# Last layer's output of an FFT network: each 32-partition quadrant holds a quarter of an image's rows, and 40 output transfers stand in place of 64

## The reference, cut to what matters

```
z = conv3x3(x, K);  z = relu(batchnorm(z));  x = x + 0.1 * conv3x3T(z, K)
x = batchnorm(x)
xh = fft2(x);  x = real(ifft2(xh * t))        # t: one real table per layer
```

## Time and profile before

| what | value |
|---|---|
| median of three runs | 795.53 us |
| profiled execution, its span | 796.84 us, 795.0 us |
| PE (TensorE matmul) busy | 748.3 us (94%) |
| DVE busy | 497.3 us (63%) |
| ACT busy | 449.3 us (57%) |
| POOL (GpSimd) busy | 95.5 us (12%) |
| `out<-Z` transfers | 60 by SP, 4 by ACT, 64 KB each |
| written to HBM | 4.19 MB |

### The profile page before, as it was taken

The page is one execution under the profiler, slowest core; times in us unless marked ns, Lnnn a source line. Parts: engine busy times, 40 slices in busy tenths (PEclk is TensorE's granted clock), DMA queues, the critical chain, the costliest instruction groups (busy, mean ns, idle before and its releaser), DMA issues.

```text
span 795.0 us, 14900 instructions
## 1 busy us (share of the span) xinstructions
PE 748.3 (94%) x6016; PEld 375.6 (47%) x6016; DVE 497.3 (63%) x911; ACT 449.3 (57%) x703; POOL 95.5 (12%) x92
## 2 busy tenths in 40 slices
PE   4788999999999999999999999999999999999993
PEld 1222333222455875324558752345587632455782
DVE  2568787765957853449578534496686333966761
ACT  0456666636745765267357652683576625826773
POOL 0357766830000000000000000000000000000000
PEclk9789999999999999989999999899999998999997
DMA  9991111248000132830000328400004273000045
GB/s 184 189 153 28 28 29 28 55 91 187 2 1 1 33 77 68 193 98 2 1 1 18 93 57 191 112 1 1 2 7 103 55 183 88 1 1 2 1 100 113
DMA packets 60133, 51.16 MB, mean 64 GB/s; under 512 B 53153, under 2 KB 53282, under 8 KB 58018
## 3 DMA queue, kind: packets, MB, share of 16 engines
q1 hardware_dynamic: 54690, 48.92, 28.7%
q10 hardware_dynamic: 5376, 1.30, 1.1%
HBM read 11.92 MB, written 4.19 MB: 20 GB/s over the span
## 4 chain that ended last, share of the span: by engine, by line
PE 84%; DVE 8%; ACT 2%; issue 2%; DMA 1%; SPq 1%; POOL 0%; DVEq 0%; ACTq 0%; POOLq 0%
PE psum L873 40%; PE psum L1054 7%; PE psum L1025 7%; PE psum L947 6%; PE psum L1043 6%; PE psum L1009 5%; PE psum L896 3%; PE psum L998 3%; DVE spare L810 2%; PE psum L973 2%; PE psum L935 2%; DVE work L810 2%; PE psum L912 1%; DVE tabT L794 1%; PE psum L1018 1%
## 5 line engine op out<-in xcount | busy, mean ns | idle before, releaser
L873 PE MATMUL psum<-Z,wts 128*32 128x512 f32 x1536 | 176.7, 613 | 1.9 <-DVE Z L787 1.9
L873 PE MATMUL psum<-X,wts 128*32 128x512 f32 x1536 | 170.1, 593 | 0.2 <-DMA X<-X 0.2
L810 DVE COPY work<-psum 64x256 f32<-64x256 f32 x224 | 100.3, 448 | 22.8 <-PE psum L1009 15.9
L720 DVE BATCH_NORM_STATS2 stats<-Z 128x6 f32<-128x512 f32 x60 | 41.6, 693 | 102.2 <-ACT Z L470 101.8
L873 PEld LDWEIGHTS psum<-Z,wts 128*32 128x32 f32 x1536 | 48.9, 112 | 116.4 <-issue 107.8
L470 ACT ACTIVATE Z<-psum 128x512 f32<-128x512 f32 x64 | 38.2, 598 | 113.2 <-PE psum L873 102.1
L873 PEld LDWEIGHTS psum<-X,wts 128*32 128x32 f32 x1536 | 47.5, 109 | 105.4 <-issue 103.0
L555 ACT ACTIVATE work<-psum 64x256 f32<-64x256 f32 x160 | 83.1, 519 | 22.4 <-PE psum L1043 15.4
L530 ACT ACTIVATE Z<-Z,small 64x128 f32<-64x128 f32 (+3 forms) x92 | 84.8, 972 | 5.2 <-DVE small L778 4.7
L801 DVE SCALAR_TENSOR_TENSOR X<-psum,X 128x512 f32<-128x512 f32 x64 | 43.8, 684 | 46.6 <-PE psum L873 46.2
L542 ACT ACTIVATE work<-psum 128x512 f32<-128x512 f32 x64 | 61.1, 1108 | 8.9 <-PE psum L998 8.8
(11 more groups left out here) (104 smaller groups left out, 897.0 us busy)
## 6 DMA issues: line engine op xcount, KB each, us to landing
X<-X SPq DMA_DIRECT2D x64, 260.0 KB, 3.8
Z<-Z SPq DMA_DIRECT2D x32, 520.0 KB, 7.1
Z<-x SPq DMA_DIRECT2D x36, 128.0 KB, 4.8
out<-Z SPq DMA_DIRECT2D x60, 64.0 KB, 1.9
parS<-par SPq DMA_DIRECT2D x4, 673.0 KB, 8.2
Z<-x SPq DMA_DIRECT2D x12, 120.0 KB, 4.9
Z<-x ACTq DMA_DIRECT2D x14, 64.0 KB, 4.3
Z<-x SPq DMA_DIRECT2D x14, 64.0 KB, 4.6
```

Of the source, the lines that this page charges most:

```text
L810: last = nc.vector.tensor_copy(dst, src)
L873: last = nc.tensor.matmul(out_b[C * r:C * r + C, :], weights[:, o:o + C], rows(src, reg, bp, g, CH, dj - 1), start=(dj == 0), stop=(dj == ...
```

## The change

In the last layer only, quadrant r holds the 16 successive rows 16r to 16r + 15 of an image in place of every fourth row.

- `back_from_h` has another destination for the last layer: `backw` is laid out as (l, r, channel, part) with h = 16r + l. The same 64 elements of a copy now go out as 4 runs (r) of 16 elements (l), with 128 floats (512 bytes) between successive elements.
- `keep_invW` writes Z2 as (image, row l, column): an image's 16 rows of a quadrant lie together, 4 KB in a run.
- `store` sends, for each quadrant, n rows of one image as one run per partition, to a DRAM stretch that is one run too. Pairs 0 to 2 are sent whole (8 transfers of 128 KB for a pair, runs of 4 KB), after all four quarters. Pair 3 is sent in halves as before (64 KB, runs of 2 KB).

```diff
-        def planar(bp, p0=0, p1=128):
-            return Z2[p0:p1, bp * REG2:bp * REG2 + G * ROW].rearrange("p (g b w) -> p g b w", b=2, w=W)
+        def leaving(bp, image, l, n, p0=0, p1=128):
+            o = bp * REG2 + G * W * image + W * l
+            return Z2[p0:p1, o:o + W * n]
...
-        def back_from_h(n, bp, q):
+        def back_from_h(n, bp, q, last):
             src = bank(n).rearrange("p (c t h) -> p t c h", c=4, t=2)
             dst = backw[bp % 2][:, :].rearrange("p (h c e) -> p e c h", c=C // 2, e=2)[:, :, 4 * q:4 * q + 4]
+            if last:
+                src = bank(n).rearrange("p (c t r l) -> p t c r l", c=4, t=2, r=R)
+                dst = backw[bp % 2][:, :].rearrange("p (l r c e) -> p e c r l", r=R, c=C // 2, e=2)[:, :, 4 * q:4 * q + 4]
...
-        def store(eng, bp, image, g0, g1):
-            for r in range(R):
-                eng.dma_start(in_dram(out, 2 * bp + image, r)[:, g0:g1],
-                              planar(bp, C * r, C * r + C)[:, g0:g1, image]).then_inc(out_done, 16)
+        def store(eng, bp, image, l, n):
+            for q in range(R):
+                to = out[2 * bp + image].rearrange("c (q l) w -> q c (l w)", q=R)[q]
+                eng.dma_start(to[:, W * l:W * l + W * n],
+                              leaving(bp, image, l, n, C * q, C * q + C)).then_inc(out_done, 16)
...
-            for bp in range(BP):
-                for h in range(2):
-                    for q in range(2 * h, 2 * h + 2):
-                        bk.result(NUMBER["invW", DEPTH - 1, bp * Q + q])
-                    for image in range(2):
-                        if (bp, h, image) != (BP - 1, 1, 1):
-                            store(sp, bp, image, G // 2 * h, G // 2 * h + G // 2)
-            sp.wait_ge(out_done, 16 * 2 * B * R)
+            for bp in range(BP - 1):
+                for q in range(Q):
+                    bk.result(NUMBER["invW", DEPTH - 1, bp * Q + q])
+                for image in range(2):
+                    store(sp, bp, image, 0, G)
+            for h in range(2):
+                for q in range(2 * h, 2 * h + 2):
+                    bk.result(NUMBER["invW", DEPTH - 1, (BP - 1) * Q + q])
+                store(sp, BP - 1, 0, G // 2 * h, G // 2)
+                if h == 0:
+                    store(sp, BP - 1, 1, 0, G // 2)
+            sp.wait_ge(out_done, 16 * (2 * R * (BP - 1) + 4 * R))
...
                 if j == DEPTH - 1:
-                    dst = planar(c // Q)[:, CH * (c % Q):CH * (c % Q) + CH]
-                    src = bank(n).rearrange("p (g w b) -> p g b w", g=CH, b=2)
+                    both = Z2[:, c // Q * REG2:c // Q * REG2 + 2 * G * W].rearrange("p (b l w) -> p l b w", b=2, w=W)
+                    dst = both[:, CH * (c % Q):CH * (c % Q) + CH]
+                    src = bank(n).rearrange("p (l w b) -> p l b w", l=CH, b=2)
```

More of the change, by code:

```diff
@@ L553, in keep_moved @@
                 bk.full(n)
-                for dst, src in forth_from_w(n, c % Q) if stage == "fwdW" else back_from_h(n, c // Q, c % Q):
+                for dst, src in forth_from_w(n, c % Q) if stage == "fwdW" else back_from_h(n, c // Q, c % Q, j == DEPTH - 1):
                     last = nc.scalar.activation(dst, src, ACT.Identity)
@@ L596, in _ @@
                 bk.result(NUMBER["invW", DEPTH - 1, (BP - 1) * Q + q])
-            store(act, BP - 1, 1, G // 2, G)
+            store(act, BP - 1, 1, G // 2, G // 2)
         @block.vector
```

## The result

Six runs of the changed kernel took 790.25 to 792.25 us, median 791.08; six of the kernel before, measured with them, had a median of 795.77. The ratio of the two is 0.9936, with a 95% interval of 0.9914 to 0.9958. The direction was as forecast. The gain, 4.7 us by the medians, is half as large again as the 3.1 that I had given, and 0.9936 x 795.53 = 790.4 lies just under my range. A later comparison gave 0.9918 (0.9894 to 0.9942).

A forecast was written before the change was run, and what follows sets the result against it. SP's issue pace was taken as the bound on the kernel's end. Fewer issues 4.1, later start -1.34 and smaller hold 0.32 gave 3.1 us gained: 795.53 - 3.1 = 792.4 us, own range 791.5 to 793.3, whole range 790.7 to 795.2.

The forecast's parts named there:

- the later start: SP's first issue of pair 2 waits for four quarters, not two: 779.25 in place of 777.91, costing 1.34 us.
- the copies with the wide stride: Last layer's 64 invH copies, now writing 512 bytes apart: 0 extra, at most 61 ns a copy.
- the Z2 writes: Writes into Z2 with runs of 64 floats on both sides: 0 extra, 777 ns with or without gaps.
- the data: 2.1 MB of pairs 2 and 3 through the DMA engines from 779.25: no cost, at most 0.2 us.
- Rival 4: Strided invH copies on DVE and ACT slow down; at twice the time 5.9 us slower, 801.4; chance 0.06.
- Rival 2: Larger transfers issue or move more slowly, 0.64 us per issue; gain only 0.5 to 2.1 us; chance 0.18.
- A hold that moves: Instruction fetch holds SP's first pair 2 issue until 780.36, costing 0.79 where it cost 1.11: 0.32 us gained.
- The row at 637.65: Earlier SP issue behind an idle spell, ending 0.36 us after a fetch; taken to show first issues are held too.
- rival 1: SP's first pair 2 issue misses the fetch's hold: gain 3.9 us, time 791.6; chance 0.20.
- the pace: SP's time per store at the end: 0.51 us, of which the issue itself is 0.466, taken as unchanged.
- the landing: Time from the start of SP's last issue until its data land: 1.9 us, with 1.7 and 3.3 as ends.
- 8 issues fewer: Pair 2 on SP issued in 8 transfers, not 16, at 0.51 us each: 4.1 us gained.

The follow-up runs named there:

- the deferred transfer: The changed kernel with the last of pair 1's eight transfers issued behind pair 2's third quarter, inside the instruction fetch; one execution, 791.23 us.

## Why the prediction was right and wrong

What it had right: the end of the program is a queue of issues on SP, 28 before and 20 after; the later start costs 1.3 to 1.4 us; the copies with the wide stride and the Z2 writes cost nothing; the data cost nothing at these run lengths. Rival 4 is refuted by the copies' 616 and 607 ns. Rival 2, with its 0.64 us an issue, is true of the kernel with 40 transfers of 256-byte runs, not of this one.

**The step that failed is "A hold that moves".** I had SP's first issue of pair 2 held to 780.36 and put 0.79 us down for it. It was not held at all: it took 0.32 us. The fetch of the changed kernel, in the DMA view of 776:778:

```profile
DMA  0000000009000000000000000000000000000000
...
q8 instruction: 1, 0.02, 3.3%
```

```profile
777.33 0.32 SPq L334 DMA_DIRECT2D out<-Z  x1
...
777.68 0.42 SPq L334 DMA_DIRECT2D out<-Z  x1
```

It begins at 776.45 and takes 3.3% of 16 engines over 2 us, 1.06, so to 777.51. By the rule that the deferred transfer showed, the first issue passes, and the second cannot end before about 777.9; it ends at 778.10 in any case. The row at 637.65, on which I built, was a first issue after a pause, but 260 KB copies of the two issues before it were on their way; that it stands for an empty queue was my reading, and it failed. Besides, a fetch has no fixed length: 1.44 us in the profile before, 0.93 to 1.37 in the others. With 1.44 the second issue would have been held, by my estimate for 0.2 us (776.45 + 1.44 + 0.4 = 778.3, against 778.10) and not 0.79. What I had as rival 1 with 0.20 was thus nearer than the forecast. Its sign was a last issue by 788.8; that issue starts at 786.33, which is 788.3 when the 2.0 us of the earlier stretch are put back.

**A second term was mis-sized: the pace.** I took 0.466 from the store's own row, since an issue had not depended on the bytes. It does not, but it depends on the number of runs, 256 before and 32 now: 0.423. From the start of SP's first issue of pair 2 to the start of its last pass 9.0 us where I had 9.54 besides the hold, though four of the intervals were 0.53 to 0.55. And the landing was 1.7 and not 1.9.

The sum of the tail, in the order of the prediction: 8 issues fewer 4.1, later start -1.4, the hold gone 1.1, pace 0.5, landing 0.2: 4.5, of 12.95 - 8.45 = 4.5. I had 4.1, -1.3, 0.3 and nothing for the last two, 3.1 in all. The 1.4 between the two sums is the hold with 0.8, the pace with 0.5 and the landing with 0.2, less 0.1 of the start; all three leaned the same way, which put the time under the range.

What I weighed too lightly is that the two parts of the change need each other. Alone, the number of transfers gave 0.2 us and the length of runs 1.0; together 4.5. I had looked at whether the new runs are slower to move, and not at whether the old ones would have allowed 128 KB per issue. They did not, twice over: the issue with 512 runs takes 0.64 us, and 128 KB per 0.51 us is 257 GB/s of demand against 193 to 216 that the 256-byte runs moved at a full share.

The rule of the Trainium skill (DMA: Bandwidth & Descriptors, "Issuing engines are not separate DMA queues"), by which initiating is usually small beside the DMA, would have given no gain. These stores are an exception to it: for 64 KB the issue took 0.42 to 0.47 us and the data 0.30 at 216 GB/s. At a tail of about 7 us the data do set the end, as the rule would have it, but even there initiating is not small: 128 KB take 0.44 us at 300 GB/s, and their issue 0.42.

## What to carry to other kernels

When a program ends in a row of small transfers, count the issues after the last computation, times the time of one issue, and set the data over the engines' rate beside it; the larger one is the bound, and merging transfers moves one only until the other takes over. Lengthen the contiguous runs together with the transfers: here each alone gave 0.2 and 1.0 us and both 4.5. Compare such tails from the end of computing, not from the whole time, when earlier stretches vary by 2 us and more from run to run.

## What the runs showed of the hardware

- Issuing a store on SP cost 0.423 us with 32 runs, 0.435 with 64, 0.466 with 256 (64 KB each, with 32 runs 64 or 128 KB alike), and 0.62 to 0.68 with 512 (128 KB) while the engines moved nothing.
- 256-byte runs of stores kept the engines at shares of 0.87 to 1.06 at 169 to 216 GB/s, 2 KB and 4 KB runs at 0.85 to 1.01 at 229 to 316.
- A 16 KB instruction fetch occupied one DMA engine for 0.93 to 1.45 us. With 32 runs the first issue into an empty queue passed in 0.32 inside a fetch; a later one that began in the fetch or less than 0.2 us before it ended 0.35 to 0.40 us after it, in six executions (0.42 became 0.65 and, beside a longer fetch, 1.85). Why the fetch holds an issue, no run here shows.
- Writes of DVE and ACT 512 bytes apart cost what 128 bytes apart cost (607 for 605 ns, 616 for 614, for 256 elements).
